# Attention and mixture-of-experts block: normed input turned by transposing transfers, second matrices' products inside the steps, new places, two score buffers in the last step

## The reference

```python
x = x + attention(layernorm(x))   # 16 heads of 16, |i - j| <= half, softmax, W_o per head, Wfc, bfc
x = x + experts(layernorm(x))

# attention: half = floor(24 + 96 * sigmoid(signal(x))) // 2, so at most 60
scores = einsum('bhqd,bhkd->bhqk', q, k) / 4
out = softmax(where(band, scores, -1e30)) @ v

# experts: the 2 of 8 with the largest gates
gating = softmax(X @ Wg + bg)
h = silu((X @ W1[e] + b1[e]) * (X @ W3[e] + b3[e]))       # 256 -> 512
mixed = sum over the two of gate * (h @ W2[e] + b2[e])    # 512 -> 256
return mixed @ Wf + bf
```

## Time and profile before

| | us |
|---|---|
| median of 3 runs | 1354.57 (1354.25 to 1356.06) |
| the profiled execution | 1353.25 |
| its span in the trace | 1351.5 |
| PE busy | 1175.3 |
| DVE busy | 970.8 |
| ACT busy | 782.4 |
| POOL busy | 605.6 |
| setup | 0 to 26.0 |
| lead up to step −1 | 26.0 to 62.8 |
| step −1 | 62.8 to 100.3 |
| steps 0 to 14 (15 steps) | 100.3 to 705.0 |
| step 15 | 705.0 to 733.4 |
| tail of the attention | 733.4 to 786.2 |
| experts | 786.2 to 1351.5 |

### The profile page before, as it was taken

One profiled execution on the slowest core, in us unless ns is written; L12 is line 12 of the kernel. 1 busy time (PEld: TensorE's weight loads), 2 busy tenths in 40 slices (PEclk: granted clock), 3 DMA queues, 4 the chain that ended last, 5 costly groups with the idle time before them and its releaser, 6 DMA issues. The chain is left out here.

```text
span 1351.5 us, 47132 instructions
## 1 busy us (share of the span) xinstructions
PE 1175.3 (87%) x18161; PEld 869.7 (64%) x18177; DVE 970.8 (72%) x2167; ACT 782.4 (58%) x1463; POOL 605.6 (45%) x648
## 2 busy tenths in 40 slices
PE   4798898888888889888888259999999999999996
PEld 2464555555555545555454148888888888888885
DVE  5345868789787877878766537777777777777775
ACT  4347776776767767677565125544555445455553
POOL 2301324546545465554535715444444444454454
PEclk9899999999999989999896679999999999999999
DMA  4875554766646666465725244656645755645554
GB/s 147 242 227 115 159 149 120 210 165 188 180 111 196 166 192 175 116 183 144 213 58 176 86 135 63 110 85 125 133 57 68 176 78 71 126 65 70 64 64 48
DMA packets 211580, 177.54 MB, mean 131 GB/s; under 512 B 115522, under 2 KB 175562, under 8 KB 211290
## 3 DMA queue, kind: packets, MB, share of 16 engines
q1 hardware_dynamic: 153482, 117.78, 34.0%
q0 software_dynamic: 25728, 34.17, 15.0%
q10 hardware_dynamic: 32208, 23.33, 6.6%
HBM read 67.99 MB, written 89.90 MB: 117 GB/s over the span
## 5 line engine op out<-in xcount | busy, mean ns | idle before, releaser
L1642 PE MATMUL p_h<-xt_parts,w_hi 128*128 128x256 f16 x1824 | 273.7, 273 | 7.3 <-DVE xt_parts L1729 6.9
L1058 DVE TENSOR_REDUCE mx<-p_max 128x4 f32<-128x496 f32 (+1 forms) x248 | 211.4, 853 | 93.2 <-PE p_max L1340 92.7
L855 ACT ACTIVATE probs<-p_exp,unscale 128x736 f32<-128x736 f32 (+1 forms) x256 | 210.3, 821 | 76.1 <-PE p_exp L1340 50.3
L1788 POOL DMA_INDIRECT out<-yw,tokens x136 | 220.7, 1623 | 45.9 <-POOL tick L1787 34.7
L1733 DVE SCALAR_TENSOR_TENSOR t<-p_h,b,t 128x256 f32<-128x256 f32 x272 | 125.8, 481 | 105.3 <-ACT t L1681 99.7
L1642 PEld LDWEIGHTS p_h<-xt_parts,w_hi 128*128 128x128 f16 x1824 | 177.4, 98 | 31.3 <-DVE t L1733 9.7
L1787 POOL TENSOR_TENSOR tick<-tick 128x1 f32<-128x1 f32 x136 | 65.4, 481 | 265.4 <-ACT yw L1698 265.4
L1681 ACT ACTIVATE t<-p_h,b,undo 128x256 f32<-128x256 f32 x272 | 142.1, 554 | 67.8 <-PE p_h L1642 62.9
L1642 PE MATMUL p_h<-xt_parts,w_lo 128*128 128x256 f16 x912 | 174.0, 273 | 0.0
L744 POOL DMA_INDIRECT routed<-rows,slots x128 | 130.5, 1020 | 38.9 <-issue 38.9
L1375 PE MATMUL p_out<-probs,v 64*32 64x184 f32 (+1 forms) x4096 | 138.1, 327 | 8.3 <-DVE out_t L1071 7.7
(11 more groups left out here) (274 smaller groups left out, 2524.3 us busy)
## 6 DMA issues: line engine op xcount, KB each, us to landing
qk_dram<-qk_hi SPq DMA_DIRECT2D x128, 128.0 KB, 2.6
qs<-qk_dram SPq DMA_DIRECT2D x64, 192.0 KB, 4.3
ks<-qk_dram SPq DMA_DIRECT2D x64, 192.0 KB, 4.3
x_in<-in_x SPq DMA_DIRECT2D x64, 128.0 KB, 3.4
qk_dram<-qk_lo SPq DMA_DIRECT2D x64, 128.0 KB, 2.4
w_mat<-in_W ACTq DMA_DIRECT2D x32, 256.0 KB
out<-x_sb SPq DMA_DIRECT2D x64, 128.0 KB
w_split<-w_first_hi SPq DMA_DIRECT2D x24, 256.0 KB
```

Source lines behind the costliest of these rows:

```text
L855: nc.scalar.activation(probs[r % 3][:, :, 0:hi - lo].rearrange("p (e s) w -> p e s w", e=2), p_exp[:, :, 0:2 * WIN].rearrange("p e (s w) - ...
L1058: nc.vector.tensor_reduce(out=maxes, in_=max_buffer(r, p_max, p_exp)[:, :, 0:2 * WIN].rearrange("p e (s w) -> p e s w", s=2)[:, :, :, 0:hi ...
L1642: last = nc.tensor.matmul(p_h[:, m % KC, k, :], w[e][a][:, k, HID * c + P * m:HID * c + P * m + P], xt[:, x, c, :], start=(n == 0 and c == ...
L1788: nc.gpsimd.indirect_dma_start(out=io["out"].rearrange("b s d -> (b s) d"), out_offset=bass.IndirectOffsetOnAxis(ap=tokens[:, b, :].bitcas ...
```

## The change

**The turned normed input.** For batches 2 to 15 the eight PE transposes, ACT's `xh` copy and DVE's `xl` subtraction are gone. ACT copies the normed rows to 16 bits (`high_x`, 128x1024), POOL subtracts (`low_x`, 128x1024), SP stores both halves to DRAM (`store_x`, two transfers) and brings them back turned (`turn_x`, two transposing transfers) into `xhl`. `xh` and `xl` are views of `xhl`. The second step of this, `turn_x`, waits for the values job of batch b − 2, the last reader of the buffer. Batches 0 and 1 keep the PE transposes.

**The second matrices.** W2 · Wf is a job `W` in `p_sh` (L1445 of the new kernel): two halves of 8 matmuls for each expert, in rounds 10 and 11 of steps −1, 1, 3, ..., 13. Its operand `w2_raw` is loaded by ACT a step and a half ahead, and ACT copies the result to `w_mat`. `late_product`, expert 0's product in the setup, `w2f_scratch` and its loads are gone. `att_t` has its own memory, `v` has two buffers, and batch 0's values are made in the lead.

**The lead.** Batch 2 is normed, split, stored and turned there; SP's transfers stand in another order.

**The places.** Nearly all tables have new entries; `QK` stands in rounds 12 to 15 and the gate jobs alone in rounds 0 and 1.

**Step 15.** Its exps take `p_exp` and `p_max` by turns, as no row maxima are left to make (`exp_buffer`), and PE waits for the exp of two rounds ago. Batch 15's low half of the routed rows is on DVE, ahead of its logits, and its high half directly behind `x2n`.

**b2_rows.** Its load (every partition gets all of 8 x 256 floats) is issued by ACT at the head of the experts, not by SP in step 15; `take_result` waits for it.

```diff
-V_AT = (-9, -8)
-T_AT = (-37, -36)
-QK_AT = (-34, -33, -32, -31)
-M_AT = (-10, -3)
-D_AT = ((20, 20), (21, 21))
+V_AT = (-8, -7)
+QK_AT = (-36, -35, -34, -33)
+M_AT = (-8, -2)
+D_AT = ((20, 21), (22, 23))
 G_AT = (32, 33)
...
-NORM2_AT = (21,)
+NORM2_AT = (27,)
...
-STACK_AT = (-29, -28, -21, -17)
-STAGE_AT = (-32, -30)
+STACK_AT = (-25, -25, -17, -19)
+STAGE_AT = (-32, -29)
...
+XHI_AT = (-45,)
+XLO_AT = (-43,)
+XST_AT = (-44, -42)
+XTR_AT = (-40, -40)
...
-LOAD_AT = (-5, -4, -3)
+LOAD_AT = (-7, -5, -14)
...
-LOW_AT = (34,)
+LOW_AT = (41,)
-SCATTER_AT = (52, 61)
-PROMPT_AT = (47, 52)
+SCATTER_AT = (50, 60)
+PROMPT_AT = (45, 49)
...
+W_AT = (-6, -5)
...
+def exp_buffer(b, n, p_max, p_exp):
+
+    return p_max if b == B - 1 and n % 2 else p_exp
...
-            for e in range(EARLY):
-                pe.wait_ge(s_w2[e], 16)
-                for k in range(KC):
-                    for c in range(NC):
-                        last = nc.tensor.matmul(p_w2f[:, e % 2, k, :], w2_t[e][:, c, P * k:P * k + P], wf[:, c, :],
-                                                start=(c == 0 and k % 2 == 0), stop=(c == NC - 1), skip_group_check=True)
-                last.then_inc(s_wf, 1)
...
-        att_t = wf[:].rearrange("p c d -> p (c d)")
+        att_t = sb("att_t", [P, S])[:]
...
+            def store_x(b, h):
+                sp.wait_ge(s_xlo, b - LEAD_BATCHES + 1)
+                wait(sp, s_xt[b % 2], 32 * (b // 2 - 1))
+                sp.dma_start(xn_dram[b % 2, FT * h:FT * h + FT, :].rearrange("(t p) r -> p t r", p=P),
+                             xr[:, 2 * h:2 * h + 2, :].bitcast(U16)).then_inc(s_xst, 16)
+
+            def turn_x(b, h):
+                sp.wait_ge(s_xst, 32 * (b - LEAD_BATCHES + 1))
+                if h == 0:
+                    filled(sp, s_full, "QK", b - 2, 3)
+                    filled(sp, s_full, "V", b - 2, 1)
+                sp.dma_start_transpose(xhl[b % 2][:, h].bitcast(U16), xn_dram[b % 2, FT * h:FT * h + FT, :]).then_inc(s_xt[b % 2], 16)
...
-            for b in range(LEAD_BATCHES):
-                stage(b, 0)
-                load_x(b + 2)
-                stage(b, 1)
-                for gk in range(2):
-                    for w in range(2):
-                        stack(b, gk, w)
+            load_x(2)
+            load_x(3)
+            for w in range(2):
+                stage(0, w)
+            for gk in range(2):
+                for w in range(2):
+                    stack(0, gk, w)
+            for h in range(2):
+                store_x(LEAD_BATCHES, h)
+            for h in range(2):
+                turn_x(LEAD_BATCHES, h)
+            for w in range(2):
+                stage(1, w)
+            for gk in range(2):
+                for w in range(2):
+                    stack(1, gk, w)
...
+            def low_x(b):
+                pool.wait_ge(s_xhi, b - LEAD_BATCHES + 1)
+                nc.gpsimd.tensor_tensor(xr[:, :, D:2 * D], xn[:], xr[:, :, 0:D], ALU.subtract).then_inc(s_xlo, 1)
...
+            def high_x(b):
+                act.wait_ge(s_xn, b + 1)
+                wait(act, s_xst, 32 * (b - LEAD_BATCHES))
+                nc.scalar.activation(xr[:, :, 0:D], xn[:], ACT.Copy).then_inc(s_xhi, 1)
...
-            def keep_late(h):
-                act.wait_ge(s_wfp, h + 1)
-                wait(act, s_w2f[h % 2], 16 * (h // 2))
-                nc.scalar.activation(out_t[:, h % 2, :], p_out[:, h % 2, :], ACT.Copy).then_inc(s_wfc, 1)
-                act.wait_ge(s_wfc, h + 1)
-                act.dma_start(io["w2f"][EARLY + h // 2, :, S * (h % 2):S * (h % 2) + S], out_t[:, h % 2, :]).then_inc(s_w2f[h % 2], 16)
+            def second_product(e, half):
+                bank, _, full = job("W", e, half)
+                act.wait_ge(s_full[bank], full)
+                wait(act, s_wlo, 3 * e)
+                nc.scalar.activation(w_mat[:, 2, S * half:S * half + S], p_sh[:, bank, :], ACT.Copy).then_inc(s_free[bank], 1)
...
                     else:
-                        act.dma_start(w_mat[:, k, HID * c:HID * c + HID], io["w2f"][e, :, HID * c:HID * c + HID]).then_inc(s_wld, 16)
+                        act.dma_start(w2_raw[:, c, :], io["W2"][e, P * c:P * c + P, :]).then_inc(s_w2, 16)
...
+            def last_low_rows():
+                b = B - 1
+                dve.wait_ge(s_hi2, b + 1)
+                nc.vector.tensor_tensor(rows[b % 3][:, :, D:2 * D], x2n[:], rows[b % 3][:, :, 0:D], ALU.subtract).then_inc(s_lo2, 1)
...
+            def operand(b):
+                if b < LEAD_BATCHES:
+                    for c in range(NC):
+                        taken(pe, s_free, "T", b, c)
+                else:
+                    pe.wait_ge(s_xt[b % 2], 32 * (b // 2))
...
-                wait(pe, s_pr, ROUNDS * b + n)
-                masked_scores(p_exp, n, ks[b % 2], qs[b % 2], 3 * HD + 1).then_inc(s_st, 1)
+                if b == B - 1 and n == 1:
+                    pe.wait_ge(s_mx, ROUNDS * B)
+                wait(pe, s_pr, ROUNDS * b + n - (1 if b == B - 1 and n else 0))
+                masked_scores(exp_buffer(b, n, p_max, p_exp), n, ks[b % 2], qs[b % 2], 3 * HD + 1).then_inc(s_st, 1)
...
-            def late_product(h):
-                n, half = h // 2, h % 2
+            def second_weights(e, half):
+                bank = shared("W", e, half)
                 if half == 0:
-                    pe.wait_ge(s_w2[n], 16)
-                wait(pe, s_wfc, h - 1)
-                if h == 1:
-                    pe.wait_ge(s_biased, 1)
+                    pe.wait_ge(s_w2, 32 * e + 32)
                 for k in (2 * half, 2 * half + 1):
                     for c in range(NC):
-                        last = nc.tensor.matmul(p_out[:, half, D * (k % 2):D * (k % 2) + D], w2_t[n][:, c, P * k:P * k + P], wf[:, c, :],
+                        last = nc.tensor.matmul(p_sh[:, bank, D * (k % 2):D * (k % 2) + D], w2_raw[:, c, P * k:P * k + P], wf[:, c, :],
                                                 start=(c == 0 and k % 2 == 0), stop=(c == NC - 1), skip_group_check=True)
-                last.then_inc(s_wfp, 1)
+                last.then_inc(s_full[bank], 1)
...
             def project(b, k):
                 n, m = "qk"[k // 2], k % 2
                 bank = shared("QK", b, k)
                 if k == 0:
-                    for c in range(NC):
-                        taken(pe, s_free, "T", b, c)
+                    operand(b)
...
+            act.wait_ge(kept["s_b2st"], 16)
+            act.dma_start(b2_rows[:].rearrange("p e d -> p (e d)"),
+                          io["b2f"].rearrange("(a e) d -> a (e d)", a=1).to_broadcast([P, NE * D])).then_inc(s_b2in, 16)
...
                 after(dve, s_yw, NB * g)
+                dve.wait_ge(s_b2in, 16)
```

230 lines of the change are left out of this document (108 added, 122 removed).

## The result

The changed kernel takes **1412.15 us** (median of 4 runs, 1408.65 to 1415.79) beside 1355.23 for the kernel before: **1.0425** times as long, 95% interval 1.0405 to 1.0445. Forecast were 1313 us, 42 less than before, and a range of 1290 to 1338; measured are 57 us more than before. The profiled execution took 1412.9 us, its span is 1411.2.

A forecast was written before the change was run, and what follows sets the result against it. PE was taken to bound the steps, busy 73.0 of 82.9 us a period. Terms of −18.5, −15, −3.5, −6 and +1.5 sum to −41.5 on 1353.25, 1311.75, as a median 1313; range 1290 to 1338.

The forecast's parts named there:

- rival (b): Steps 0 to 14 give nothing, as POOL's added subtractions hold DVE ahead of row maxima: 14 us back, 1327; chance 0.17.
- step 2: Steps 0 to 14: a two-step period of 80.9 us instead of 82.9, −15 us; ends 0 and −37.5.
- The turned operand: Transposing transfers before round 12's projection: 5.8 us of room against 6.0 needed, taken as 0, ends 0 and +1.5 a batch.
- rival (d): Turned operand late to round 12, stopping PE in 13 steps; decides from 3.2 us a batch, 1365 at 4 us; chance 0.09.
- Lead, −18.5: Setup, lead and step −1: first exp of step 0 at 81.8 instead of 100.3; ends −10 and −24.
- sign of a falling clock: Lead: a PE clock that falls in the emptier lead was named as something that would show the prediction wrong; no size given.
- Step 15, −3.5: Step 15: with two buffers PE's scores and ACT's exps overlap, −3.5 us; ends 0 and −8.
- Tail, −6: Tail after the last exp: earlier reading of batch 15's variance, shorter `lg` subtraction and gates moved, −6 us; ends −2 and −9.
- term of 3.3 us: Tail: POOL, busy with scatters, reads batch 15's variance 3.3 us after it is ready; counted as a saving.
- term of 1.8 for `lg`: Tail: DVE's subtraction for `lg`, 1.97 us beside POOL's low rows against 0.19 without, counted as 1.8 saved.
- Experts, +1.5: Experts: loading the rows of b2, 1 MB, beside the first tiles' transfers costs 1.5 us; ends 0 and +4.5.
- rival (a): Whole kernel: all terms as reckoned, 1313 us, its own range 1296 to 1329; chance 0.60.

The follow-up runs named there:

- run without the chain: Changed kernel without high and low halves, stores and transposing transfers of the turned input for batches 3 to 15 (result not right): 1340.4 us, ratio 0.9892.
- statistics' run of the fourth group: Changed kernel with the second half of the first statistics in round 3 instead of round 5: 1366.2 us, ratio 1.0053 to the kernel before.

## Why the prediction was wrong

**The step that failed is 2, with its cover.** I let POOL's 4.1 us a period "go into the gaps" since POOL would stand at 47.8 of 81 us, and made rival (b) a thing of chance: "if half of the 14 new ones stand in the way", 14 us. Its mechanism was right; I never asked what stands beside the instruction. The order of the two queues shows it: POOL's `low_x` is at entry −43 and the end of the first statistics at −59, both round 5 of a step. So they stand side by side in each of the twelve steps that have both, and in nine of them they met. And the price of one meeting was not the 2.06 us of a POOL instruction: it was up to 3.8, as two POOL instructions followed each other, and PE's standstill of 4.63 and its slower clock behind it came on top. The nine holds alone are 31.7 us, and one of the gates 4.5. Hence 46 us for something I had bounded by 29. The Trainium skill's rule ("SBUF — State Buffer", section "Who interferes with whom") is that the one of DVE and GpSimd that issues first gets the shared port pair for its whole instruction and the other waits. The hold of L1040 through `low_x` agrees with it. That L1040 was still held through the next one, which POOL began at 429.41, 1.65 us behind DVE's 427.76, does not follow from it. What the section says of `tensor_scalar`, that it can take the second port too, is what I left out when I looked only at operations with two inputs.

**Also in step 2: gaps of 9.9 us that should shrink to 7.0.** The run without the chain shows 603.2 us for steps 0 to 14 instead of 604.7. Its window, with the columns of the earlier trace rows:

```profile
90.05:693.20 603.15, 539.67 (x12075) 327.40 (x12111) 453.48 (x1039) 423.68 (x661) 276.53 (x281) 0.98 0.60 158
```

The gaps did shrink: PE was idle for 63.5 us there and for 80.6 in the same steps of the kernel before (busy 524.1), which is 2.3 us a period less where I had 2.9. The term that was mis-sized is PE's work. I had it grow by 0.9 us a period, from 73.0 to 73.9, and it grew by 2.1. And I read the gaps too generously: the 9.0 us in 13 waits are those of PE's weight loads, which overlap its matmuls. PE itself waited 5.4 us of its 9.9 for the row maxima in the same two steps:

```profile
PE p_max L1333 <- DVE mx L1058: 5.4, 9, 2.0
```

**The turned operand, costed 0 with +1.5 as its end, rival (d).** Room 5.8 us, need 6.0, I wrote; measured were 7.2 from issue to projection, and waits of up to 2.5 us, 11.2 to 12.3 us in all, mostly in even steps; in odd ones the products lie between. That is 0.9 us a batch. With the copies, stores and turns around it the chain cost 19 us, 1.5 a batch. The mechanism was right and its size within the ends; 3.2 us a batch, the point at which it alone would turn the sign, was not reached.

**Lead, −18.5; measured −13.5.** The first score came at 50.0, 2.5 sooner than the 62.8 − 7.8 − 2.5 of my terms. The transfers of batch 2 lost that again, in SP's queue of the changed kernel:

```profile
48.97 1.10 SPq L615 DMA_DIRECT2D xn_dram<-xr  x2
58.28 2.70 SPq L623 DMA_TRANSPOSE xhl<-xn_dram  x2
61.03 1.28 SPq L634 DMA_DIRECT2D qk_dram<-qk_hi  x2
...
74.96 1.23 SPq L645 DMA_DIRECT2D ks<-qk_dram  x2
```

The waits in it, SP's for the stores and, at 77.12, PE's for the stack:

```profile
SPq L623 <- DMA xn_dram<-xr: 8.1, 1, 8.1
PE p_max L1367 <- DMA ks<-qk_dram: 10.3, 2, 8.1
```

The term that was mis-sized is the wait for the stores, 2.5 us: it took from 50.07 to 58.28, 8.2, at a DMA share of 0.81, with batch 1's staging behind it. In the run with PE transposes, which has no such transfers, the first exp came at 81.1. The sign of a falling clock showed as well: it was 0.52 from 50.07 to 58.28. But it was 0.52 and 0.50 from 50 to 60 in that other run too, so it does not explain the 5 us.

**Step 15, −3.5; measured 0** in the changed kernel's step, and 0 in the time of the run with this part alone. I treated the step's exps as the path. With that part alone the step was 4.7 us shorter in the trace, more than forecast, with the clock at 1.00 instead of 0.55; but the tail behind it waits for POOL's queue, and lost it again. In the changed kernel the same queue stands ahead of the exps themselves, through L844.

**Tail, −6; measured −2.3.** POOL reads the variance of batch 15 not sooner but later:

```profile
809.91 0.16 DVE L1031 TENSOR_SCALAR var<-mv 128x4 f32<-128x4 f32 x1
...
812.80 2.41 DVE L1174 TENSOR_TENSOR one<-pick,first 128x32 f32<-128x32 f32 x1
813.09 2.07 POOL L782 TENSOR_TENSOR rows<-x2n,rows 128x1024 f16<-128x1024 f32 x1
815.11 1.05 POOL L725 TENSOR_TENSOR rs<-var,neg_half 128x4 f32<-128x4 f32 x1
```

5.0 us after it is ready, against 3.3 in the earlier trace rows, since batch 14's low rows were moved behind the scatters (`LOW_AT`) and now stand ahead of it. That is the term of 3.3 us, which became a loss of 1.8. The scatters that hold POOL until then are batch 13's, by their order in the queue, not batch 14's as I wrote. The term of 1.8 for `lg` came true:

```profile
824.72 0.19 DVE L1151 TENSOR_TENSOR lg<-lg,gm 128x32 f32<-128x32 f32 x1
```

**Experts, +1.5; measured 0**: no time of b2's load shows in the span of 565.3 us.

**The range of rival (a)**, 1296 to 1329, does not come out of its own rule: with the ends of lead and steps taken half way it is 1299 to 1325. The forecast does not hang on it.

## What to carry to other kernels

When work is moved to an engine that is half idle, read the other engine's queue at the same place: what counts is which instruction stands beside it in each period, not the two busy shares. In a schedule written by hand such a meeting repeats from period to period, so its price is the number of meetings times the hold and what stands still behind it, and a single table entry can undo most of it. Making one stage shorter is worth nothing if another engine's queue sets when the next stage starts: look at what reads the last result of the stage, and how long that result had lain ready. A time that was won on one chip should be measured on a second before it is believed: here the sign of the change hung on it.

## What the runs showed of the hardware

- A DVE instruction can be passed over by more than one POOL instruction: 3.81 us for one of 0.17, over two of 2.14 and 2.13 back to back. In the statistics' run of the fourth group a 128x32 instruction got in between the same two and took 1.93 us. In the run with the subtraction on DVE, L1038's row starts 0.31 us ahead of POOL's and is 2.43 us long all the same. In the changed kernel bn_stats and the row maxima that start beside such POOL instructions keep their length (0.41 us for each bn_stats, 0.93 for a row maximum of 128x736).
- Two transposing transfers of 256 rows of 512 16-bit numbers (eight 128x128 blocks each) take 5.09 us on the queue and 7.2 us from the first issue to the reader, with the DMA engines at a share of 0.95 in that time.
- Behind a standstill of 4.63 us the granted clock of PE was 0.54 for 3 us, and the next product took 0.86 us instead of 0.54.
- The kernel before took 1355 to 1357 us beside the changed kernel and in the first, fourth and fifth group, and 1453 and 1460 in two others on other chips. The traces of the changed kernels on those show most DVE, ACT and POOL instructions of the same length and stops of PE within a product; of the kernel before there is no trace there. On a chip of the latter kind the changed kernel was 0.7% faster, on one of the former 4.3% slower.
